# One level of Strassen's algorithm in the square matmul of a conditioned FFN kernel on one core

## What is computed

```
W = cond_weights[condition]                      # (64, 64, 64)
y = einsum('bct,bcd->bdt', x, W)                 # 4096 tokens of 1024 features
logits = y @ gate_w.T + expert_bias;  one_hot = one_hot(argmax(logits))
base_out = y @ W_up.T                            # 4096 x 1024 x 1024, fp32
z = y @ lora_A.T;  delta = (z of the chosen expert) @ lora_B
out = x + base_out + delta
```

## Time and profile before

| | |
|---|---|
| time, median of 3 runs | 479.15 us (478.44 to 479.24) |
| span of the profiled execution, first to last instruction | 476.6 us |
| what lies around it, median less span | 2.6 us |
| TensorE busy | 468.1 us, 98% |
| VectorE, ScalarE, GpSimd busy | 266.6, 165.9 and 5.3 us |
| granted clock of TensorE, mean | 0.996 |
| HBM traffic | 81 GB/s over the span |

### The profile page before, as it was taken

The page is one execution under the profiler, slowest core; times in us unless marked ns, Lnnn a source line. Parts: engine busy times, 40 slices in busy tenths (PEclk is TensorE's granted clock), DMA queues, the critical chain, the costliest instruction groups (busy, mean ns, idle before and its releaser), DMA issues.

```text
span 476.6 us, 8204 instructions
## 1 busy us (share of the span) xinstructions
PE 468.1 (98%) x3064; PEld 464.8 (98%) x3065; DVE 266.6 (56%) x532; ACT 165.9 (35%) x245; POOL 5.3 (1%) x19
## 2 busy tenths in 40 slices
PE   8899999999999999999999999999999999999997
PEld 7799999999999999999999999999999999999996
DVE  3888555556655455655555665555566554556322
ACT  4765333323333322333332233333233333223110
POOL 2100000000000000000000000000000000000000
PEclk9899999999999999999999999999999999999999
DMA  9802211222220122222022222102222201221111
GB/s 251 346 0 90 89 52 38 89 89 88 90 88 36 52 88 88 88 88 65 33 77 88 88 88 88 50 38 88 88 88 88 88 34 54 88 89 44 45 45 44
DMA packets 12911, 38.75 MB, mean 81 GB/s; under 512 B 3358, under 2 KB 3742, under 8 KB 12898
## 3 DMA queue, kind: packets, MB, share of 16 engines
q1 hardware_dynamic: 11698, 38.02, 22.7%
q0 software_dynamic: 160, 0.28, 0.3%
q10 hardware_dynamic: 1040, 0.26, 0.2%
HBM read 21.78 MB, written 16.78 MB: 81 GB/s over the span
## 4 chain that ended last, share of the span: by engine, by line
PE 94%; DVE 3%; DMA 1%; ACT 1%; issue 0%; SPq 0%
PE out_ps L367 78%; PE y_ps L312 11%; PE out_ps L376 4%; DMA cond_sb<-in_L_cond_weights_dram 1%; PE out_ps L331 1%; DVE wl L433 1%; PE out_ps L389 1%; DVE lora_b_hl L439 0%; DVE yl L422 0%; DVE y_sum L415 0%; ACT yh L247 0%; DVE cond_hl L475 0%; ACT cond_hl L266 0%; ACT wh L262 0%; ACT y_small L239 0%
## 5 line engine op out<-in xcount | busy, mean ns | idle before, releaser
L367 PE MATMUL out_ps<-wh,yh 128*128 128x354 f32 (+1 forms) x768 | 251.6, 328 | 0.8 <-DVE wl L433 0.8
L367 PE MATMUL out_ps<-wh,yl 128*128 128x354 f32 (+1 forms) x768 | 249.3, 325 | 0.0
L367 PE MATMUL out_ps<-wl,yh 128*128 128x354 f32 (+1 forms) x768 | 248.7, 324 | 0.0
L367 PEld LDWEIGHTS out_ps<-wh,yh 128*128 128x128 f32 x768 | 145.1, 189 | 1.0 <-issue 1.0
L367 PEld LDWEIGHTS out_ps<-wl,yh 128*128 128x128 f32 x768 | 145.0, 189 | 0.0
L367 PEld LDWEIGHTS out_ps<-wh,yl 128*128 128x128 f32 x768 | 144.6, 188 | 0.0
L239 ACT ACTIVATE y_small<-y_ps 128x512 f32<-128x512 f32 x64 | 38.3, 598 | 174.5 <-PE y_ps L312 174.4
L415 DVE TENSOR_TENSOR y_sum<-y_ps,y_small 128x512 f32<-128x512 f32 x64 | 44.0, 688 | 83.2 <-ACT y_small L239 83.2
L410 DVE TENSOR_TENSOR x_hl<-x_sb,x_hl 64x1024 fp32r<-64x1024 f32 x64 | 78.1, 1220 | 7.9 <-ACT x_hl L234 6.0
L422 DVE TENSOR_TENSOR yl<-y_sum,yh 128x512 fp32r<-128x512 f32 x64 | 44.3, 693 | 44.9 <-ACT yh L247 44.8
L234 ACT ACTIVATE x_hl<-x_sb 64x1024 fp32r<-64x1024 f32 x64 | 67.3, 1051 | 2.5 <-DMA x_sb<-in_x_dram 1.7
(11 more groups left out here) (35 smaller groups left out, 92.3 us busy)
## 6 DMA issues: line engine op xcount, KB each, us to landing
x_sb<-in_x_dram SPq DMA_DIRECT2D x32, 512.0 KB, 4.0
out_dram<-out_sb SPq DMA_DIRECT2D x31, 512.0 KB, 2.9
w_up_sb<-in_L_ffn_W_up_dram SPq DMA_DIRECT2D x8, 512.0 KB, 12.2
cond_sb<-in_L_cond_weights_dram ACTq DMA_DIRECT2D x1, 256.0 KB, 5.1
cond_sb<-in_L_cond_weights_dram SPq DMA_DIRECT2D x1, 256.0 KB, 5.8
out_dram<-out_sb SPq DMA_DIRECT2D x1, 177.0 KB, 2.6
out_dram<-out_sb SPq DMA_DIRECT2D x1, 176.0 KB, 1.9
out_dram<-out_sb SPq DMA_DIRECT2D x1, 159.0 KB, 2.0
```

What stands on the lines that cost most here:

```text
L367: mm = pe.matmul(bank, y[:, s % 2, k, :], w[:, k, a:b], start=(k == 0 and y is yh and w is wh), stop=(k == KC - 1 and y is yl))
```

## The change

Two pairs (256 tokens, `t` = 0 and 1) now form a block, and 16 blocks are worked. The block's y is a 2 by 2 matrix of 128x512 pieces (a11, a12 for the first tile, a21, a22 for the second), and the weight is a 2 by 2 matrix of 512x512 pieces. Instead of eight piece products there are seven, in Winograd's form of Strassen's algorithm. The operands of y are a11, a12, a22, s1 = a21 + a22, s2 = s1 - a11, s3 = a11 - a21 and s4 = a12 - s2, and each has its own weight combination, prepared once in `w_of`. Each operand is split into high and low (`round_operand` on ScalarE, `low_operand` on VectorE). Four operands (`ROUTED`) also carry the 36 router columns: their product is two matmuls per chunk and split part, of 292 and 256 columns, and the others' is one of 512.

The sums s1 to s4 are made by GpSimd. The outputs are put together in place on the loaded x: `p1` (the product of a11, copied out of PSUM by ScalarE) is added to x by GpSimd, VectorE adds the products that lie in PSUM to x or to `p1` (`add_c11`, `add_p5`, `add_u2`, `add_p4`, `add_c12`, `add_u3`), and GpSimd adds the growing `p1` to the remaining parts of x. There is no `out_sb`; a store starts from the x buffer, and the next x is loaded into it once the store has landed. The weight combinations are made in the opening, on GpSimd (`add_t`, three adds for each of four chunks) and VectorE (four adds), and 28 groups of weight transposes take the place of 16; each group's copy and subtraction are as before. None of them stands between matmuls of a product any more.

Shortened to its core (comments with # name the engine):

```diff
-    PAIRS = B // 2
-    COLS = GC + O
-    PARTS = 3
-    EDGES = [0, 354, 708, COLS]
+    BLOCKS = B // 4
...
+    OPS = ["a11", "a12", "a22", "s1", "s2", "s4", "s3"]
+    ROUTED = ["a11", "a12", "a22", "s1"]
...
+        def in_blocks(eng, period):
+            period(0, 0, True, False)
+            with eng.Fori(0, BLOCKS // 2 - 1) as group:
+                for n in range(2):
+                    period(group * 2 + (n + 1), (n + 1) % 2, False, False)
+            period(BLOCKS - 1, (BLOCKS - 1) % 2, False, True)
...
+        def x_part(par, t, half):
+            return x_sb[:, 2 * par + t, half * BANK:(half + 1) * BANK]
...
+        GROUPS = [("a11", c) for c in range(OH)] + [("gate", 0)] + [("a12", c) for c in range(OH)] \
+            + [("lora", h) for h in range(2)]
+        FIRST = len(GROUPS)
+        for op in ("s1", "a22", "s2", "s4", "s3"):
+            GROUPS += [(op, c) for c in range(OH)]
...
 # SyncE
+            def period(q, par, opening, closing):
+                sp.wait_ge(c11_out, q + 1)
+                sp.dma_start(out_pairs[2 * q, :, 0:BANK], x_part(par, 0, 0)).then_inc(stored[0], 16)
+                sp.wait_ge(c12_out, q + 1)
+                sp.dma_start(out_pairs[2 * q, :, BANK:O], x_part(par, 0, 1)).then_inc(stored[0], 16)
+                if not closing:
+                    sp.wait_ge(stored[0], 32 * q + 32)
+                    load(q, par, 0)
...
 # GpSimd
+            def add_s1(q):
+                pool.wait_ge(y_summed, 4 * q + 4)
+                pool.tensor_tensor(s_sum[:, :], a21[:, :], a22[:, :], ALU.add).then_inc(s1_added, 1)
+            def add_s2(q):
+                pool.wait_ge(low["s1"], q + 1)
+                pool.tensor_tensor(s_sum[:, :], s_sum[:, :], a11[:, :], ALU.subtract).then_inc(s2_added, 1)
+            def add_s4(q):
+                pool.wait_ge(s2_added, q + 1)
+                pool.wait_ge(low["a12"], q + 1)
+                pool.tensor_tensor(a12[:, :], a12[:, :], s_sum[:, :], ALU.subtract).then_inc(s4_added, 1)
+            def add_s3(q):
+                pool.wait_ge(s1_added, q + 1)
+                pool.tensor_tensor(a21[:, :], a11[:, :], a21[:, :], ALU.subtract).then_inc(s3_added, 1)
+            def add_t(c):
...
+            def period(q, par, opening, closing):
+                if not opening:
+                    pool.wait_ge(low["s2"], q)
+                    add_s1(q)
+                add_s2(q)
+                pool.wait_ge(p1_copied, 2 * q + 2)
+                pool.tensor_tensor(wide(x_part(par, 0, 0)), wide(x_part(par, 0, 0)), p1[:, :, 0:QUARTER], ALU.add)\
+                    .then_inc(p1_added, 1)
+                add_s4(q)
+                add_s3(q)
+                pool.wait_ge(u2_out, q + 1)
+                pool.tensor_tensor(wide(x_part(par, 0, 1)), wide(x_part(par, 0, 1)), p1[:, :, 0:QUARTER], ALU.add)\
+                    .then_inc(u2_added, 1)
+                pool.wait_ge(u3_out, q + 1)
+                for half in range(2):
+                    pool.tensor_tensor(wide(x_part(par, 1, half)), wide(x_part(par, 1, half)), p1[:, :, 0:QUARTER],
+                                       ALU.add).then_inc(u3_added, 1)
...
 # ScalarE
+            def period(q, par, opening, closing):
+                if not opening:
+                    move_small_y(q, 1, 1)
+                    round_a22(q, opening)
+                    round_s1(q, opening)
+                    copy_p1(q, opening)
+                round_s2(q, opening)
+                round_s4(q, opening)
+                round_s3(q, opening)
...
 # TensorE
+                    pe.wait_ge(turned_low, LAST_OF[op])
+                w = w_of[op]
+                if op in ROUTED:
+                    pieces = [(bank[:, 0, 0:QUARTER + GC], slice(0, QUARTER + GC)),
+                              (bank[:, 1, 0:QUARTER], slice(QUARTER + GC, BANK + GC))]
+                else:
+                    pieces = [(bank, slice(0, BANK))]
+                for k in range(KH):
+                    for a, b in ((0, 0), (0, 1), (1, 0)):
+                        for dst, cols in pieces:
+                            mm = pe.matmul(dst, hl[op][:, a, k, :], w[:, b, k, cols],
+                                           start=(k == 0 and a + b == 0), stop=(k == KH - 1 and a == 1))
+                mm.then_inc(product_done[op], 1)
...
+                if not opening:
+                    pe.wait_ge(c12_out, q)
+                    multiply("a11", bank_x, q, opening)
+                    pe.wait_ge(u3_out, q)
+                    multiply("a12", bank_y, q, opening)
+                    pe.wait_ge(p4_out, q)
+                else:
+                    pe.wait_ge(turned_low, len(GROUPS))
+                    pe.wait_ge(gate_diff_low, 1)
+                multiply("a22", bank_z, q, opening)
+                if opening:
+                    pe.wait_ge(y_summed, 4)
+                turn_z(y_ps[:, 0, 0:P], q, 0)
+                pe.wait_ge(p1_copied, 2 * q + 2)
+                multiply("s1", bank_x, q, opening)
+                pe.wait_ge(z_ready, 2 * q + 1)
+                for n in range(2):
+                    mm = add_delta(0, bank_y[:, n, 0:QUARTER], lora_b_hl[:, n * QUARTER:(n + 1) * QUARTER])
+                mm.then_inc(delta11, 1)
+                if not closing:
+                    make_y(q + 1, 0, 0, False, index)
+                pe.wait_ge(c11_out, q + 1)
+                multiply("s2", bank_y[:, 0, :], q, opening)
+                pe.wait_ge(p5_out, q + 1)
+                turn_z(bank_x[:, 1, 0:P], q, 1)
+                if not closing:
+                    make_y(q + 1, 0, 1, False, index)
+                pe.wait_ge(z_ready, 2 * q + 2)
+                if opening:
+                    pe.wait_ge(lora_diff_low, 1)
+                for n in range(2):
+                    mm = add_delta(1, bank_z[:, n, 0:QUARTER], lora_d_hl[:, n * QUARTER:(n + 1) * QUARTER])
+                mm.then_inc(delta21, 1)
+                multiply("s4", bank_x[:, 0, :], q, opening)
+                add_delta(0, bank_x[:, 0, :], lora_b_hl[:, BANK:O]).then_inc(delta12, 1)
+                if not closing:
+                    make_y(q + 1, 1, 0, False, index)
+                multiply("s3", bank_y[:, 1, :], q, opening)
+                add_delta(1, bank_y[:, 1, :], lora_b_hl[:, BANK:O]).then_inc(delta22, 1)
+                if not closing:
+                    make_y(q + 1, 1, 1, False, index)
+            in_blocks(pe, period)
...
 # VectorE
+            def add_c11(q, par):
+                dve.wait_ge(delta11, q + 1)
+                dve.wait_ge(p1_added, q + 1)
+                dve.tensor_tensor(wide(x_part(par, 0, 0)), bank_y[:, :, 0:QUARTER], wide(x_part(par, 0, 0)), ALU.add)\
+                   .then_inc(c11_out, 1)
+            def add_p5(q, par):
+                dve.tensor_tensor(wide(x_part(par, 1, 1)), bank_x[:, :, 0:QUARTER], wide(x_part(par, 1, 1)), ALU.add)
+                dve.tensor_tensor(wide(x_part(par, 0, 1)), bank_x[:, :, 0:QUARTER], wide(x_part(par, 0, 1)), ALU.add)\
...
+            def add_u3(q):
+                dve.wait_ge(delta22, q + 1)
+                dve.tensor_tensor(p1[:, :, 0:QUARTER], wide(bank_y[:, 1, :]), p1[:, :, 0:QUARTER], ALU.add)\
+                   .then_inc(u3_out, 1)
...
+            def period(q, par, opening, closing):
+                if not opening:
+                    sum_y(a22, q, 1, 1)
+                    low_operand("a22", a22, q)
+                    low_operand("s1", s_sum, q)
+                    add_partial(q, 0)
+                if opening:
+                    route(q, 0, opening)
+                low_operand("s2", s_sum, q)
+                low_operand("s4", a12, q)
+                if not opening:
+                    route(q, 0, opening)
+                low_operand("s3", a21, q)
+                if not closing:
+                    split_x(q + 1, 1 - par, 0)
+                add_c11(q, par)
+                add_partial(q, 1)
+                route(q, 1, opening)
+                if not closing:
+                    sum_y(a11, q + 1, 0, 0)
+                add_p5(q, par)
+                if not closing:
+                    low_operand("a11", a11, q + 1)
+                add_u2(q)
+                if not closing:
+                    split_x(q + 1, 1 - par, 1)
+                    sum_y(a12, q + 1, 0, 1)
+                add_p4(q, par)
+                if not closing:
+                    low_operand("a12", a12, q + 1)
+                add_c12(q, par)
+                if not closing:
+                    sum_y(a21, q + 1, 1, 0)
+                add_u3(q)
+            in_blocks(dve, period)
```

More of the change, by code:

```diff
@@ L170, in _ @@
+        lora_right = a22[:, 0:OH * (P // 2)].rearrange("q (j p) -> q j p", j=OH)
+        lora_left = a21[:, :]
+        LOW_ROWS = slice(2 * ER, 4 * ER)
         @block.sync
@@ new lines, in load @@
+            def load(q, par, t):
+                sp.dma_start(x_sb[:, 2 * par + t, :], x_pairs[2 * q + 4 + t]).then_inc(x_loaded[2 * par + t], 16)
```

(65 more changed lines are left out.)

637 lines of the change are left out of this document (368 added, 269 removed).

## The result

The changed kernel takes 583.13 us (median of 4 runs, 581.25 to 584.31), the kernel before on the same chip 479.16: ratio 1.218, interval 1.215 to 1.221. It is slower by 104 us. The forecast was 547 with a range of 505 to 590.

What follows compares the result with a forecast made beforehand. TensorE's work bounded the kernel before; the change would be bound by a chain over GpSimd's adds with port cost. Span 62 + 15 x 30.8 + 20.3 = 544.3, plus 2.6 around it: 547 us, range 505 to 590.

Steps and rivals of the forecast that it cites:

- The signs named: GpSimd adds near 1.1 us, TensorE some 80% busy, `turn_z` waits about 3 us, VectorE waiting for ScalarE, ScalarE for GpSimd.
- What it removes: TensorE's matmuls per block: own work falls from 28.0 to 25.0 us, 48 us over 16 blocks.
- the chain hidden, 460: Rival: adds and routing hide behind a11, a12, a22; TensorE bounds, period near 25.0 us, time 460; chance 0.06.
- The add: GpSimd's 128x512 add of two SBUF operands: 1.1 us taken, between 0.74 and 1.42; six in the chain.
- The port: GpSimd adds meeting two-SBUF-operand VectorE instructions: four meetings in the chain at 0.46 us, 1.9 us a block.
- My next sentence: At the shared port, VectorE held as well: some 3 us a block instead of 1.9, 18 us more in time.
- The part ahead of the chain: From a block's first `turn_z` to its last delta: 14.95 us plus waits of 1.2 and 0.35, so 16.5.
- TensorE's clock falls in each block: Rival: idle stretches in each block lower TensorE's clock, say 1.5 us a block, time 569; chance 0.27.
- Opening: Start to first `turn_z`: 62 us, before 33.64; last chunk's t1 at 45.6, 17 groups 11.7, a22 3.1.
- No cost at the port: Rival: the chain's GpSimd and VectorE meetings fall where there is slack; period 28.9, time 519; chance 0.22.

Runs made afterwards that it cites:

- the run with four adds: Changed kernel with s1 to s4 added by VectorE, p1, u2, u3 left on GpSimd, VectorE's and ScalarE's lists reordered: 494.13 us, 1.033 of the kernel before.
- the run without them: Changed kernel with the low parts of a22, s1, s2, s4 reading a PSUM bank instead of their SBUF operand: 548.65 us, 1.148 of the kernel before.
- the warm run: Changed kernel with 16 unread identity transposes on TensorE ahead of the first tile's z transpose, from the second block on: 568.74 us, 1.190 of the kernel before.

## Why the prediction was right or wrong

The direction, the mechanism and the range held; the time was 36 us low. The signs named came: adds near 1.1 us and longer beside VectorE, TensorE 81% busy, waits of 2.9 us for the routing, and VectorE waiting for ScalarE, which waits for GpSimd. The profiled span of 582.5 is 66.8 + 15 x 32.85 + 22.9, where the sum was 62 + 15 x 30.8 + 20.3. Of the 38 us between them 17 are the period at full clock, 13.4 the fallen clock in the blocks, 4.8 the opening and 2.6 the end, the last nearly all the clock's too.

**What it removes, half right.** A routed product costs what was forecast, 3.14 us for 3.07 in the chain of the changed kernel (start, us, what):

```profile
262.97 0.33 PE y_ps L582
263.30 3.14 PE bank_x L573 x24
```

But "TensorE's own work falls from 28.0 to 25.0 us" was too good: in the run with four adds y halves, deltas and transposes took 5.0, not 4.6, and s2 to s4 8.5, not 8.2, together 25.8. And the change reads four indices at a stroke, which I had not counted: 1.26 us more. TensorE's own period is 27.1 there, so 0.9 us a block, 14 over 15 blocks and not 48, were to be had, less than half of what the opening loses. The rival "the chain hidden, 460" was out of reach for this reason too.

**The add, mis-sized.** 1.1 us was taken, 1.28 measured (bounds 0.74 and 1.42). Six in the chain are 1.1 us a block. The Trainium skill (GPSIMD Engine Reference, Elementwise — side-by-side cycle accounting) measures about 2.6 cycles an element for a two-input add, from which my estimate was 1.11 us. The traces do not bear it out, with 1.28 for an add that meets nobody; the measurement decides.

**The port, right in kind.** One meeting does cost an add 0.46 us (1.74 against 1.28). I forecast 1.9 us a block on the chain; the run without them shows 1.3, for two adds and part of two low parts, not four meetings. VectorE is held too, 1.09 for 0.69, which I had left out of the sum. The Trainium skill (SBUF — State Buffer, SBUF: two separate sides) says that the loser of the shared port pair waits for the whole instruction. The trace of the run with four adds agrees: s2 takes 1.79 us and ends 0.55 behind the add of 1.31 that began 0.07 before it. My next sentence, that this would make it 3 us, was too much: in the chain's meetings only part of the other's instruction was left to wait for.

**The part ahead of the chain, mis-sized.** At full clock (the warm run) the last delta ends 17.9 us behind `turn_z`, forecast 16.7: part of the 0.8 of TensorE's own work above, and longer waits. From there to the next `turn_z` it is 14.1, as forecast, but by luck: the adds were 1.1 dearer, the meetings 0.6 cheaper, and what else was 0.5 cheaper I have not traced. So 30.8 became 31.96, 17 us in all.

**The clock, left out of the sum.** I left "TensorE's clock falls in each block" as a rival at 0.27 with 1.5 us a fall. It fell in 9 of 15 at 1.5 each, 13.4 us, and cost 2.5 at the end (22.9 against 20.4 in the warm run). I had judged a product-filled first part a reason against it. Each of the nine falls came 0.5 to 1.5 us behind a `turn_z` that had waited 2.6 to 2.9 us. Five more had waited as long and no fall followed, so these waits alone do not say where it falls.

**Opening.** 66.8 against 62. The t1 of the last chunk ended at 48.6, not 45.6: five of the ten adds took 1.27 us and five, beside VectorE, 1.6 to 1.7, together 14.6 for 11, with fewer handoffs than allowed. The groups behind it took 13.1 us for 11.7; the a22 product ran at clock 0.50, 4.8 us for 3.1.

**"No cost at the port", 519.** False as a description of this kernel, but it names part of the remedy: with the chain's meetings and the falls gone it is 549, and with s1 to s4 and u3 out of GpSimd's chain 494.

What stays open: why one reading of four registers stalls TensorE by 0.8 to 1.7 us where two at a time, in the kernel before, leave no gap, and why the stall alternates (0.88 and 1.61) in some runs and not in others. A kernel with two readings at a time was not tried. Nor was the opening shortened, so no version here beats the kernel before. By the sum alone, an estimate, the one with four adds would with an opening under 49.7 us for its 65.5, since it is 15.8 us behind.

## What to carry to other kernels

Fewer multiplications pay only if the additions that replace them have somewhere to lie: draw the chain from one product through every add, rounding and routing to the next before counting what TensorE saves. The same eight adds cost 583, 547, 516 or 494 us by where they ran and in what order they stood, more than the saving itself. Put an add of two SBUF operands on GpSimd only where VectorE reads one operand from PSUM beside it, and where no small instruction of the chain, such as the routing, runs. Allow for a fallen clock where the chain leaves TensorE waits: with waits of 2.6 to 2.9 us it fell in 9 of 15 blocks here and cost 13.4 us.
